# First projections at full height, the middle tile in four 64x64 tiles, five of a norm's twelve term copies on GpSimd, and a new order of steps

## The reference, cut to what matters

```python
x = _L0_conv_ref(x, ...)      # inverted bottleneck, expert weights mixed per image by a router
x = _L1_conv_ref(x, ...)
t = _to_tokens(x)             # 3136 tokens of 24 channels
t = t + _L2_attn_ref(_ln_t(t), ...)   # linear attention, 6 heads
t = t + _L2_ffn_ref(_ln_t(t), ...)    # fp8 feed-forward, hidden 96
t = t + _L3_attn_ref(_ln_t(t), ...)   # Fourier mixing: fft, diagonal, inverse fft
t = t + _L3_ffn_ref(_ln_t(t), ...)
```

```python
rw = jax.nn.sigmoid(pooled @ Wr + br)                # routing weights from the pooled image
Wk = jnp.einsum('be,ecm->bcm', rw, Wpw)
h = jnp.einsum('bhwc,bcm->bhwm', x, Wk) + (rw @ bpw)[:, None, None, :]   # 24 -> 96
h = jax.nn.relu(_bn(h, g1, b1, m1, v1))
h = _cond_dw(h, Wdw, bdw, rw)                        # 3x3 depthwise
h = jax.nn.relu(_bn(h, g2, b2, m2, v2))
h = jnp.einsum('bhwm,bmf->bhwf', h, Wk2) + ...       # 96 -> 24
return _bn(h, g3, b3, m3, v3) + shortcut
```

## Time and profile before

| | before |
|---|---|
| median of 3 runs | 2684.66 us (2683.72 to 2687.61) |
| the profiled execution's own time | 2684.42 us |
| its span, first to last instruction | 2682.3 us |
| PE busy | 2305.7 us (86%) |
| DVE busy | 1948.2 us (73%) |
| ACT busy | 1678.5 us (63%) |
| POOL busy | 69.0 us (3%) |
| mean granted TensorE clock | 0.880 |

### The profile page before, as it was taken

How to read it: one execution, slowest core, us unless ns; L and a number is a source line. 1 busy time by engine, 2 the same in 40 slices (tenths; PEclk the granted TensorE clock), 3 DMA queues, 4 the chain that set the end, 5 groups by cost and what they waited for, 6 DMA issues and landing times.

```text
span 2682.3 us, 49164 instructions
## 1 busy us (share of the span) xinstructions
PE 2305.7 (86%) x19776; PEld 1278.3 (48%) x19776; DVE 1948.2 (73%) x3879; ACT 1678.5 (63%) x2824; POOL 69.0 (3%) x130
## 2 busy tenths in 40 slices
PE   3776988999889997999889998899879998987765
PEld 2233434664336733555336743465335553563552
DVE  4884977788857896697948788587866989466243
ACT  3344457756667567766856667766766668657654
POOL 1000000000000000000000000000000000000000
PEclk9887979989879897899879898899887998978766
DMA  4001001000020002000020000100010000000000
GB/s 132 1 1 19 1 1 19 2 2 1 1 36 2 1 1 37 2 1 1 1 37 2 1 1 2 36 2 1 1 28 2 2 1 1 20 1 1 19 1 19
DMA packets 108593, 29.56 MB, mean 11 GB/s; under 512 B 104144, under 2 KB 104272, under 8 KB 107984
## 3 DMA queue, kind: packets, MB, share of 16 engines
q1 hardware_dynamic: 108368, 26.41, 4.9%
HBM read 16.77 MB, written 9.63 MB: 10 GB/s over the span
## 4 chain that ended last, share of the span: by engine, by line
PE 59%; DVE 20%; ACT 12%; issue 4%; SPq 3%; DMA 1%; ACTq 0%; DVEq 0%
PE P L720 12%; PE P L701 9%; DVE acc L1417 7%; PE P L765 6%; PE P L915 4%; PE P L737 4%; PE P L741 3%; PE P L928 3%; SPq L574 2%; PE P L956 2%; PE P L756 2%; DVE SQ L1558 2%; PE P L866 2%; PE P L779 2%; PE P L940 1%
## 5 line engine op out<-in xcount | busy, mean ns | idle before, releaser
L1417 DVE SCALAR_TENSOR_TENSOR acc<-H,Dm,acc 128x784 f32<-128x784 f32 x1024 | 991.3, 1028 | 86.7 <-ACT acc L1083 86.3
L701 PE MATMUL P<-T,Wk 48*128 48x448 f32 (+5 forms) x768 | 402.5, 626 | 40.4 <-ACT H L1076 19.9
L720 PE MATMUL P<-H,diag 64*64 64x392 f32 x4608 | 401.0, 498 | 5.8 <-DVE T L1433 5.7
L1076 ACT ACTIVATE H<-P,biasA 128x448 f32<-128x448 f32 (+1 forms) x384 | 235.7, 621 | 216.2 <-PE P L701 145.9
L720 PEld LDWEIGHTS P<-H,diag 64*64 64x64 f32 x4608 | 171.5, 134 | 215.0 <-issue 201.9
L765 PE MATMUL P<-T,pack_b 112*112 112x448 f32 x448 | 245.0, 637 | 21.3 <-ACT mid L1124 6.6
L701 PEld LDWEIGHTS P<-T,Wk 64*128 64x128 f32 (+2 forms) x768 | 128.1, 205 | 177.5 <-ACT H L1076 73.8
L1106 ACT ACTIVATE acc<-P,biasT 128x392 f32<-128x392 f32 x128 | 69.1, 584 | 181.2 <-PE P L720 181.2
L1083 ACT ACTIVATE acc<-H,Dm 128x784 f32<-128x784 f32 x128 | 121.4, 949 | 49.5 <-PE P L741 47.2
L737 PE MATMUL P<-acc,Wk 64*112 64x392 f32 x256 | 118.7, 587 | 28.7 <-ACT acc L1112 28.6
L1433 DVE SCALAR_TENSOR_TENSOR T<-P,bias,T 112x392 f32<-112x392 f32 x128 | 78.6, 623 | 80.3 <-PE P L741 79.1
(11 more groups left out here) (192 smaller groups left out, 3800.7 us busy)
## 6 DMA issues: line engine op xcount, KB each, us to landing
xin<-in_x SPq DMA_DIRECT2D x224, 42.0 KB, 2.2
out_y<-arena SPq DMA_DIRECT2D x8, 1176.0 KB, 6.0
pack_b<-in_pack_b SPq DMA_DIRECT2D x1, 3820.5 KB, 17.4
arena<-in_pack_s SPq DMA_DIRECT2D x1, 1548.0 KB, 8.5
pack_a<-in_pack_a SPq DMA_DIRECT2D x1, 1084.0 KB, 5.3
pack_i<-in_pack_i SPq DMA_DIRECT2D x1, 320.0 KB, 3.1
arena<-in_pack_k SPq DMA_DIRECT2D x1, 192.0 KB, 3.2
```

The source lines that it names most:

```text
L701: pe.matmul(conv_rows(slice(0, 128), HB[(NP * s + e) % len(HB)], n), Wk1[rows, 128 * j:128 * (j + 1)], image_rows(T[q % 3][rows, :], a, n) ...
L720: last = pe.matmul(conv_rows(slice(64 * h, 64 * (h + 1)), CVB + r, HH), diag[64 * r:64 * (r + 1), tap, :], H1[64 * r:64 * (r + 1), slot(s, ...
L1076: act.activation(H1[:, slot(s, j), o:o + n, 1:1 + HW], conv_rows(slice(0, 128), HB[(NP * s + e) % len(HB)], n), ACT.Relu, bias=biasA[:, j, ...
L1417: ins = ve.scalar_tensor_tensor(a, H1[:, slot(s, j), r:r + SR, c:c + HW], Dm[:, j, tap:tap + 1], a, ALU.mult, ALU.add)
```

## The change

- `hidden` reads all 112 rows of `T` for each of the three tiles. The rows of the weight that belong to other images are zero (`maskI`), so the values stay.
- `conv_out` becomes two steps. The first waits for `t2_ready` alone and issues the middle tile's four matmuls as 64x64 tiles: channels of image 1 go to output rows 0 to 63, those of image 2 to rows 64 to 111, none accumulates onto another. The second waits for `h2_ready` and issues the four matmuls of tiles 0 and 2 as before.
- In a norm, the four copies of the high term and the first of the middle term move to POOL, in a new step `shift_terms`, each waiting for the one before. DVE keeps seven. PE's first spreading matmul waits for `rs_shifted` too. Two DVE signals get semaphores of their own.
- The lists in `TURNS` are written anew for all four engines.

```diff
--- before.py
+++ after.py
@@ -82,119 +82,121 @@
 
 TURNS = {
     "gpsimd": (
-        "d7 b2 c11 m1 c10 m1 c5 b1 c4 b1 c3 m1 c3 b1 c4 b1 c2 m1 c4 b1 c4 b1 c2 m1 c4 b1 c4 b1 c2 m1 c4 b1 c4 "
...
+        "d7 b1 c10 m1 c1 m1 c5 m1 c4 b2 c2 m2 c4 b2 c1 m1 c4 b2 m1 c1 m1 c3 b1 c1 b1 m1 c4 b2 c1 m1 c1 m1 c4 "
...
     ),
     "tensor": (
...
     ),
     "scalar": (
...
     ),
     "vector": (
...
     ),
 }
 
@@ -445,7 +447,7 @@
         in_tp = sig("in_transposed", NCK)
         in_evac = sig("in_evacuated", NCK)
         chain_c = sig("vector_chain_conv", 2 * (5 + NV * (len(VE_TAPS) - 1)))
-        chain_m = sig("vector_chain_middle", 5 + 4 + 5)
+        chain_m = sig("vector_chain_middle", 3 + 4 + 3)
         pw_ready = sig("pooled_weights_ready", 2)
         lg_psum = sig("logits_in_psum", 2)
         lg_ready = sig("logits_ready", 2)
@@ -471,7 +473,9 @@
             norm.sq_ready = sig(f"squares_ready_{half}", layers * NCK)
             norm.var_psum = sig(f"variance_in_psum_{half}", layers * NCK)
             norm.sd_ready = sig(f"deviation_ready_{half}", layers)
+            norm.term_ready = [sig(f"{name}_terms_ready_{half}", layers) for name in ("high", "middle")]
             norm.rs_ready = sig(f"rstd_ready_{half}", layers)
+            norm.rs_shifted = sig(f"rstd_shifted_{half}", (LT + 1) * layers)
             norm.rs_psum = sig(f"rstd_in_psum_{half}", layers * NCK)
             norm.y_ready = sig(f"normalised_ready_{half}", layers * NCK)
 
@@ -515,7 +519,7 @@
         wt_ready = sig("turned_ready", NTR)
         fo_psum = sig("fourier_out_in_psum", NFO)
         fo_added = sig("fourier_added", NFO)
-        chain_b = sig("vector_chain_back", 2 * 5 + NSG)
+        chain_b = sig("vector_chain_back", 2 * 3 + NSG)
 
         ot_psum = sig("out_in_psum", NCK)
         ot_ready = sig("out_ready", NCK)
@@ -538,6 +542,10 @@
             return t[:, :].rearrange("c (y x) -> c x y", x=HW)
 
         Y_x = by_column(Y)
+
+        def shift(eng, norm, k, t):
+
+            return eng.tensor_copy(norm.thirds[32 * k:32 * (k + 1), t, :], norm.terms[k][32 * t:32 * (t + 1), :])
 
         def every(program):
             for q in range(NQ):
@@ -633,12 +641,24 @@
             def conv_end(q):
                 yield
 
+            def shift_terms(q, norm, i):
+                yield
+                hold(pool_e, norm.term_ready[0], norm.term_ready[0].at(q, i + 1))
+                for t in range(LT):
+                    shift(pool_e, norm, 0, t).then_inc(norm.rs_shifted.sem, 1)
+                    pool_e.wait_ge(norm.rs_shifted.sem, norm.rs_shifted.at(q, (LT + 1) * i + t + 1))
+                pool_e.wait_ge(norm.term_ready[1].sem, norm.term_ready[1].at(q, i + 1))
+                shift(pool_e, norm, 1, 0).then_inc(norm.rs_shifted.sem, 1)
+                pool_e.wait_ge(norm.rs_shifted.sem, norm.rs_shifted.at(q, (LT + 1) * (i + 1)))
+
             def middle(q):
+                yield from shift_terms(q, normM, 0)
                 yield
                 hold(pool_e, normM.y_ready, normM.y_ready.at(q, NCK))
                 pool_e.memset(YT[:, :, RC:RC + 1], 1.0).then_inc(ones_ready.sem, 1)
                 pool_e.wait_ge(ones_ready.sem, ones_ready.at(q, 1))
                 pool_e.memset(bdw[2][:, 0:PAD], 0.0).then_inc(ones_ready.sem, 1)
+                yield from shift_terms(q, normM, 1)
 
             def back(q):
                 yield
@@ -648,11 +668,13 @@
                 hold(pool_e, normB.y_ready, normB.y_ready.at(q, 0))
                 pool_e.memset(arena[96:128, reg1:reg1 + TOK], 1.0).then_inc(fpads_set.sem, 1)
                 pool_e.wait_ge(fpads_set.sem, fpads_set.at(q, 1))
+                yield from shift_terms(q, normB, 0)
                 yield
                 hold(pool_e, out_stored, out_stored.at(q, 16))
                 for n, dst in enumerate((arena[:, reg1 + TOK:reg1 + 64 * HW], Hf[:, :, HW:64])):
                     pool_e.memset(dst, 0.0).then_inc(fpads_set.sem, 1)
                     pool_e.wait_ge(fpads_set.sem, fpads_set.at(q, n + 2))
+                yield from shift_terms(q, normB, 1)
 
             for_quads("gpsimd", conv_part, conv_end, middle, back)
 
@@ -697,9 +719,8 @@
                             pe.wait_ge(cw_ready.sem, cw_ready.at(q, L + 1))
                         else:
                             pe.wait_ge(h1_ready.sem, h1_ready.at(q, max(NP * L * NS, NP * (L * NS + s) + e + 1 - len(HB))))
-                        rows = {0: slice(0, 64), TJ: slice(0, R), 2: slice(64, R)}[j]
-                        pe.matmul(conv_rows(slice(0, 128), HB[(NP * s + e) % len(HB)], n), Wk1[rows, 128 * j:128 * (j + 1)],
-                                  image_rows(T[q % 3][rows, :], a, n), start=True, stop=True).then_inc(h1_psum.sem, 1)
+                        pe.matmul(conv_rows(slice(0, 128), HB[(NP * s + e) % len(HB)], n), Wk1[:, 128 * j:128 * (j + 1)],
+                                  image_rows(T[q % 3], a, n), start=True, stop=True).then_inc(h1_psum.sem, 1)
 
             def taps(q, L, s):
 
@@ -729,13 +750,14 @@
 
                 yield
                 pe.wait_ge(t2_ready.sem, t2_ready.at(q, 2 * (L * NS + s + 1)))
-                pe.wait_ge(h2_ready.sem, h2_ready.at(q, L * NV + 2 * (s + 1)))
-                for r in range(2):
+                for r, out_rows in enumerate((slice(0, 64), slice(64, R))):
                     for h in range(2):
                         rows = slice(64 * h, 64 * (h + 1))
                         w = Wk2p[rows, TJ * RC:TJ * RC + R] if r == h else Wk2t[rows, :]
-                        pe.matmul(conv_rows(slice(0, R), CVB + h, HH), w,
-                                  image_rows(acc[rows, (NT * s + TJ) % N2, :], HH * r, HH), start=(r == 0), stop=False)
+                        pe.matmul(conv_rows(out_rows, CVB + h, HH), w[:, out_rows],
+                                  image_rows(acc[rows, (NT * s + TJ) % N2, :], HH * r, HH), start=True, stop=False)
+                yield
+                pe.wait_ge(h2_ready.sem, h2_ready.at(q, L * NV + 2 * (s + 1)))
                 for h in range(2):
                     for j, out_rows, w in ((0, slice(0, 64), Wk2p[:, 0:64]), (2, slice(64, R), Wk2[:, 2, 2 * CH:RC])):
                         last = pe.matmul(conv_rows(out_rows, CVB + h, HH), w, image_rows(acc[:, (NT * s + j) % N2, :], HH * h, HH),
@@ -772,6 +794,7 @@
                 for c in range(NCK):
                     yield
                     if c == 0:
+                        pe.wait_ge(norm.rs_shifted.sem, norm.rs_shifted.at(q, (LT + 1) * (i + 1)))
                         pe.wait_ge(norm.rs_ready.sem, norm.rs_ready.at(q, i + 1))
                     if c >= NSP:
                         pe.wait_ge(norm.y_ready.sem, norm.y_ready.at(q, N0 + c - NSP + 1))
@@ -1442,13 +1465,14 @@
                 link(ve.reciprocal(norm.rstd, norm.sdev), q, half)
 
                 rest, (high, middle_, low) = norm.sdev, norm.terms
-                link(ve.tensor_copy(high, norm.rstd), q, half)
+                ve.tensor_copy(high, norm.rstd).then_inc(norm.term_ready[0].sem, 1)
+                ve.wait_ge(norm.term_ready[0].sem, norm.term_ready[0].at(q, i + 1))
                 link(ve.tensor_tensor(rest, norm.rstd, high, ALU.subtract), q, half)
-                link(ve.tensor_copy(middle_, rest), q, half)
+                ve.tensor_copy(middle_, rest).then_inc(norm.term_ready[1].sem, 1)
+                ve.wait_ge(norm.term_ready[1].sem, norm.term_ready[1].at(q, i + 1))
                 link(ve.tensor_tensor(low, rest, middle_, ALU.subtract), q, half)
-                for k, term in enumerate(norm.terms):
-                    for t in range(LT):
-                        last = ve.tensor_copy(norm.thirds[32 * k:32 * (k + 1), t, :], term[32 * t:32 * (t + 1), :])
+                for k, t in ((1, 1), (1, 2), (1, 3), (2, 0), (2, 1), (2, 2), (2, 3)):
+                    last = shift(ve, norm, k, t)
                 last.then_inc(norm.rs_ready.sem, 1)
                 for c in range(NCK):
                     yield
```

3 lines of the change are left out of this document (2 added, 1 removed), and 211 rows, old and new, of the table TURNS.

## The result

The changed kernel takes **2538.09 us** (median of 4 runs, 2534.74 to 2539.51) against 2684.36 us for the kernel before (4 runs, 2683.72 to 2687.61): ratio **0.9451, 95% interval 0.9435 to 0.9467**. It is faster, by 147 us where 55 were forecast, and outside the range on its lower side. The profiled execution took 2539.51 us.

A forecast was written before the change was run, and what follows sets the result against it. PE was taken to bound the conv work with DVE close behind, and long dependent stages the tail. Matmul edits -61, norm -8 and order +14 gave -55 us against 2684.4: forecast 2630 us, range 2565 to 2680.

The forecast's parts named there:

- The order: New lists: 14 us later in the tail from moved norm steps; within a quad nothing counted, 25 us either way.
- The clock, held at 0.88: PE's mean granted clock kept as profiled, turning 93 us at full clock into 105 us of PE busy time.
- The middle tile: Second projection: four matmuls take 0.83 us instead of 1.51, 44 us less over 64 strips, bounds 0 and 53.
- The two matmul edits: PE's projections: 105 us less busy time, 76 on the path, a fifth off for DVE: 61 us less.
- The full height: First projections of tiles 0 and 2: 256 matmuls, each 0.19 us shorter, 49 us less, bounds 5 and 69.
- The norm: Five copies fewer on DVE in 32 norms: 31 us of DVE time, counted at 0.27 as 8 us less.
- The split: conv_out in two steps: the same wait, moved to the second half; nothing counted, 14 us at best.
- POOL against DVE: Shared SBUF interfaces: POOL's copies could hold DVE for up to 48 us; left out of the sum.
- Nearly all of it shows: Rival, whole kernel: new lists fitted to shorter steps keep PE as full, 2572 to 2585 us; chance 0.22.
- DVE takes over: Rival, conv work: PE's gain turns into waits for taps, 2665 us; chance 0.18 together with tiles not overlapping.
- the tiles don't overlap: Rival, middle tile: matmuls don't run four at a time, 34 us lost, 2664 us; 0.18 together with DVE bounding.
- the clock went the other way: Rival, PE: more gaps lower the granted clock; gain gone at mean 0.84, 2714 us at 0.82; chance 0.08.

The follow-up runs named there:

- f_only: The kernel before with only the full-height first projections, in the old order: 2636.77 us, ratio 0.9809.
- m_only: The kernel before with only the middle tile in four 64x64 tiles, one step behind both waits, old order: 2660.85 us, ratio 0.9893.
- fm_only: The kernel before with full-height projections and the middle tile's 64x64 tiles, second projection still one step, old lists: 2609.01 us, ratio 0.9690.
- c_only: The kernel before with five copies of each norm on POOL and the second projection in two adjacent steps, old lists: 2659.25 us, ratio 0.9885.
- order_only: The kernel before with its own operations in the new lists, the middle tile's old matmuls in their own step: 2620.83 us, ratio 0.9758.
- ops_only: The kernel before with all operations of the change, POOL's copies too, in the old lists: 2581.73 us, ratio 0.9594.
- c7: The change with seven of a norm's twelve copies on POOL, without waits between them: 2533.48 us, ratio 0.9419 to the kernel before.
- c8: The change with eight of a norm's twelve copies on POOL, without waits between them: 2533.40 us, ratio 0.9416 to the kernel before.

## Why the prediction was wrong

The sign was right; the forecast of 55 us is 92 short of 147. By the ratios, from the kernel before: both matmul edits 83 us, the split 3, the copies 23, the new lists 38. By PE's time in the profiled executions (us; a minus is less than in the kernel it is compared with):

| | span | PE work | cost of the low clock | idle |
|---|---|---|---|---|
| full height (`f_only`) | -47 | -18 | -50 | +21 |
| middle tile (`m_only`) | -22 | -45 | +12 | +11 |
| both (`fm_only`) | -76 | -62 | -44 | +29 |
| copies (`c_only`) | -31 | 0 | -17 | -14 |
| new lists (`order_only`) | -78 | -1 | -48 | -29 |
| new lists on all operations (`ops_only` to the change) | -43 | +8 | -40 | -10 |
| the change | -145 | -56 | -86 | -3 |

**The order: the step that failed.** "Within a quad the same steps stand in a different mesh, and I count nothing, with 25 us either way", with +14 us for the tail. The lists gave -38 us, tail included: 52 us of the miss. The tail was read right (forecast +14, the windows show +20 to +24). What the prediction had wrong is that another order of the same steps leaves PE's time as it is: the lists took 40 us off what the low clock costs and 10 us off PE's idle time, with 8 us more work. It also did not count which steps leave the conv work for the handover. The earlier trace rows had both prices: conv work, where PE is at 93% and DVE at 84%, and a handover with PE at 81%, DVE at 38% and the clock at 0.70. The part of the order that I compared was one strip and the tail; counting one quad's steps would have shown the feed-forward leave. It would not have given the clock.

**The clock, held at 0.88.** The sum turns PE's time into busy time "with mean 0.88", and the clock has a price only as a rival that falls, since the low phases are "the handover and the tail, where the change takes little out". It rose to 0.907, and 161 of the 168 us less at the low level (added up from the clock record) lie ahead of the tail. What it is worth can be read from runs: over 36 executions of the kernel before, whose mean clock lay between 0.875 and 0.887, the span is 19 us shorter for each 0.01 more (14 in the prediction). By that, 0.027 more are an estimated 52 us of time; PE's busy time has 86 us of it. Two parts go with it: the full height (96 us less at the low level, by all executions 102 in the old order and 69 in the new one) and the new lists (92, by all executions 84; on top of the operations 85 both ways). The middle tile did not. The copies' 34 us less in `c_only` (26 by all executions) are within what executions differ by.

**The two matmul edits.** The prediction had 93 us at full clock, 105 of busy time, and with 0.6 and 0.85 of it on the path and a fifth off for DVE -61; measured -83: 22 us. That PE busy fell by 105.6 us in `fm_only`, just as forecast, is luck: it is 62 us of work and 44 of clock. The middle tile was sized right (44 forecast; 45 in the old order, 38 in the new one). The full height was not: 18 us for 49. The rows compared a 48-row matmul whose neighbours on both sides have another form (0.95) with a 112-row one whose neighbours have its own (0.76). In both kernels it is the changes of form that cost. Call two neighbours of one form when their rows and columns lie in the same class (up to 32, up to 64, more), and take the projections with 448 columns at full clock with no gap on either side. A full-height one takes 0.75 us (median) with no change beside it, 0.86 with one, 0.95 with two; a tiled one 0.95 with two, 0.86 with one and 0.75 with none (nine and five cases). Of the tiled ones before, 122 of 136 had two changes; of the full-height ones in the change 87 have none, 86 one and 41 two. So full height saves 0.1 or 0.2 us only where its neighbours have its form. Its 51 us of time are the clock's for the greater part, so the measured 51 us beside the forecast 49 does not bear the estimate out. And taking something off for DVE had a ground: PE's idle time rose by 29 us in `fm_only`, and DVE's share of the chain to 31%.

**The norm.** The sizes held (0.28 us a copy on POOL, DVE busy 1921.6 against 1917 forecast, PE waiting for DVE). The 0.27 was too low: it divides DVE's share of the chain by its busy share, an average over a line of taps that waits for PE and a line of copies of which half is on the path. For L701 and L737 the prediction took the line's own share; for L1451 that gives 0.52 x 31 = 16 us. Measured 14 to 31, so that is nearer. The taps queue behind the copies on DVE, which may be the rest; no run shows it alone. 15 us of the miss.

**The split.** "I count nothing" held: 3 us by itself. "It is the same wait" did not: with the step split in the old order the idle time fell from 28.4 us to 12.0 already, and in the change it is 16.8. A wait that shrinks on PE was worth next to nothing here.

**POOL against DVE.** The prediction gave up to 48 us for contention, by the rule of the Trainium skill, "GPSIMD Engine Reference", section 8. For the instructions that it names, those with two SBUF inputs, the trace of the change shows nothing, as no tap of DVE's runs beside a copy of POOL's; in `c7` and `c8` 18 and 24 taps do, with 1.037 and 1.053 us against 1.027 and 1.028 for the others. The 224 copies left on DVE take 28.2 + 22.9 = 51.1 us, 10.6 more than at the 0.181 of before, but not evenly. Most keep 0.18 us with POOL's copy beside them; the first of a set takes 0.21 and the fourth 0.31, ending just behind POOL's copy; and twelve take 0.44 and 0.78 us beside two memsets of POOL's (L675), which make 5 of the 10.6 us. In the kernel before no copy took over 0.19. DVE's busy time fell by 26.6 us net in the change.

**The rivals.** "Nearly all of it shows" (2572 to 2585 us) has the time of `ops_only`, 2581.73, in its range, and PE did stay about as full there (384.0 us idle against 376.6); but 46 of the 109 us that its busy time fell by are the clock, which this rival had not moved either. It too counted nothing for the order. That DVE takes over and that the tiles don't overlap are refuted, and the clock went the other way.

## What to carry to other kernels

Before you read a gain off PE's busy time, take it apart: what the matmuls need at full clock, what the low clock adds, and idle time. Here more than half of a gain that looked like shorter matmuls was the clock. Compare two forms of a matmul between the same neighbours, and take the median of many and not the best row. Price a step by its own line's share of the chain, not by its engine's: a short serial piece between two engines is on the path even where its engine is not. Where a schedule is rewritten, count for every period, from one fixed step to the same step of the next, which steps leave the stretch in which two engines are full, and for where; here two stretches won 109 us in all and two others lost 46.

## What was not expected of the hardware

- A change of form beside a float32 matmul of 448 columns costs 0.1 us on each side, whichever form it has: 0.75 us from start to next start with no change, 0.86 with one, 0.95 with two (medians at full clock). The tiled form by itself costs nothing that shows, in the few cases without a change.
- Full height instead of 64- and 48-row tiles took 96 us off PE's time at the low clock (644 to 548) while PE's idle time rose by 21 us (376.6 to 397.7, span less busy time); half of the edit took 66 us off. New lists for the same operations took 92 us off while idle time fell by 29 us. The middle tile in four 64x64 tiles, with PE's idle time 11 us longer, took nothing off (26 us more in the profiled execution, 14 by all). So neither less waiting nor less work by itself raised the clock. What does stays open.
- Four 64x64 matmuls of 392 columns with nothing to accumulate take 0.81 us, where two pairs that accumulate took 1.51.
- A small DVE copy of 32 x 112 elements keeps its 0.18 us beside most of POOL's copies, takes 0.31 where it starts just behind the start of one, and 0.44 and 0.78 beside memsets of POOL's of 0.48 and 0.74 us, just behind which it ends. A POOL copy takes 0.33 us from start to next start, whether it waits for the one before (0.28 us long) or not (0.33 long, `c7`, `c8`): the waits cost nothing.
